# Gate/up in parts, two ff2 tiles after gru, and a split pointwise product in a one-core recurrent block

## The reference, cut to what matters

```
xn   = layernorm(x)
s    = recurrent(xn)      # conv + pointwise, minGRU, feed-forward, each with rmsnorm and residual
gate = fp4(xn) @ fp4(w_gate).T
up   = fp4(xn) @ fp4(w_up).T            # both 704 columns
h    = silu(gate) * up
g    = silu(fp4(h) @ fp4(w_down).T)
out  = x + s * g

def fp4(v):               # per block of 16 along the last dimension
    scale = max(max|v| / 6, 1e-12)
    return round_to_grid(v / scale, [0, .5, 1, 1.5, 2, 3, 4, 6]) * scale
```

## Time and profile before

| | us |
|---|---|
| median of 3 runs (lowest to highest) | 1191.91 (1191.78 to 1193.99) |
| the profiled execution | 1193.24 |
| its span, first to last instruction | 1191.2 |
| PE busy | 1102.8 (93%) |
| DVE busy | 865.2 (73%) |
| ACT busy | 549.9 (46%) |
| POOL busy | 143.1 (12%) |
| mean granted TensorE clock | 0.979 of full |

### The profile page before, as it was taken

How to read it: one execution, slowest core, us unless ns; L and a number is a source line. 1 busy time by engine, 2 the same in 40 slices (tenths; PEclk the granted TensorE clock), 3 DMA queues, 4 the chain that set the end, 5 groups by cost and what they waited for, 6 DMA issues and landing times.

```text
span 1191.2 us, 18158 instructions
## 1 busy us (share of the span) xinstructions
PE 1102.8 (93%) x6306; PEld 969.6 (81%) x6306; DVE 865.2 (73%) x1638; ACT 549.9 (46%) x887; POOL 143.1 (12%) x122
## 2 busy tenths in 40 slices
PE   3467999999999999999999999999999999999998
PEld 2355988879898888988888798987889888888987
DVE  5777686868868586885868678686777858777655
ACT  3235454454545455453545444454444434544441
POOL 3010020101102010110201011020201101020010
PEclk9587999999999999999999999999999999999999
DMA  6000000010101001010010101001010100100000
GB/s 225 1 0 18 19 27 28 1 55 1 36 18 34 22 1 53 1 36 20 1 53 1 54 1 36 19 1 55 1 36 17 36 19 1 53 1 18 18 19 18
DMA packets 29355, 31.46 MB, mean 26 GB/s; under 512 B 1120, under 2 KB 28512, under 8 KB 29280
## 3 DMA queue, kind: packets, MB, share of 16 engines
q1 hardware_dynamic: 20000, 21.04, 5.6%
q10 hardware_dynamic: 9280, 9.26, 2.4%
HBM read 21.90 MB, written 8.39 MB: 25 GB/s over the span
## 4 chain that ended last, share of the span: by engine, by line
PE 76%; DVE 15%; issue 4%; ACT 4%; DMA 0%; POOL 0%; DVEq 0%; ACTq 0%; POOLq 0%
PE gu_ps L855 39%; PE w_ps L855 26%; PE w_ps L918 3%; DVE hqt_lo L471 2%; DVE x L506 2%; DVE hq L393 2%; DVE q_amax L367 2%; PE gu_ps L901 1%; PE w_ps L862 1%; ACT hqt_hi L732 1%; PE w_ps L873 1%; PE gu_ps L862 1%; DVE q_y L379 1%; PE w_ps L901 1%; DVE cand L504 1%
## 5 line engine op out<-in xcount | busy, mean ns | idle before, releaser
L855 PE MATMUL w_ps<-w,act 128*128 128x256 f32 x960 | 217.1, 379 | 0.0
L455 DVE TENSOR_TENSOR hid<-sl,gu_ps 128x352 f32<-128x352 f32 x128 | 65.7, 514 | 189.2 <-ACT sl L721 189.1
L855 PEld LDWEIGHTS w_ps<-w,act 128*128 128x128 f32 x960 | 177.7, 190 | 21.7
L855 PE MATMUL gu_ps<-gu_hi,xq_hi 128*128 128x352 f32 x512 | 170.1, 332 | 10.5 <-issue 9.5
L855 PE MATMUL gu_ps<-gu_lo,xq_hi 128*128 128x352 f32 x512 | 166.7, 326 | 1.7 <-issue 1.6
L855 PE MATMUL gu_ps<-gu_hi,xq_lo 128*128 128x352 f32 x512 | 166.4, 325 | 0.0
L855 PE MATMUL w_ps<-dn_hi,hqt_hi 128*128 128x256 f32 x384 | 119.6, 312 | 8.6 <-DVE hqt_lo L471 8.6
L721 ACT ACTIVATE sl<-gu_ps 128x352 f32<-128x352 f32 x128 | 59.4, 464 | 133.9 <-PE gu_ps L855 133.5
L327 POOL TENSOR_TENSOR inv_rms<-ss_row,neg_half 128x4 f32<-128x4 f32 x32 | 40.6, 1270 | 596.3 <-DVE ss_row L481 596.3
L759 ACT ACTIVATE act<-gu_ps,cols 128x512 f32<-128x512 f32 x128 | 86.5, 688 | 54.7 <-PE gu_ps L855 54.6
L855 PE MATMUL gu_ps<-xs_hi,w_hi 128*128 128x512 f32 x256 | 106.2, 415 | 3.1 <-DVE xs_lo L495 3.1
(11 more groups left out here) (115 smaller groups left out, 2199.4 us busy)
## 6 DMA issues: line engine op xcount, KB each, us to landing
x_in<-x_dram SPq DMA_DIRECT2D x16, 512.0 KB, 4.5
x_res<-x_dram ACTq DMA_DIRECT2D x16, 512.0 KB, 3.5
out_dram<-o SPq DMA_DIRECT2D x15, 512.0 KB, 3.2
act<-w_t_dram SPq DMA_DIRECT2D x1, 1024.0 KB, 13.3
w<-w_t_dram SPq DMA_DIRECT2D x1, 1024.0 KB, 15.6
act<-w_down_dram SPq DMA_DIRECT2D x1, 704.0 KB, 10.3
hid<-w_gate_dram SPq DMA_DIRECT2D x1, 640.0 KB, 5.6
hid<-w_up_dram SPq DMA_DIRECT2D x1, 640.0 KB, 9.2
```

The lines of the kernel that those rows point to most:

```text
L455: V.tensor_tensor(hid[:, t, h * HALF:(h + 1) * HALF], sl[:, h, :], gu_ps[:, h, 1, 0:HALF], ALU.mult).then_inc(hid_ready, 1)
L855: done = M.matmul(psum, l, r, start=first and i == 0, stop=last and i == len(terms) - 1)
```

## The change

1. `gate_up(c, t, u)`: a call now does one part u (0 gate, 1 up) over all 704 columns, that is both halves, each half in a bank of its own. The bank indices are swapped to `gu_ps[:, u, h]`. The gate part waits for the silu of the tile before, the up part for its product. Silu and product are one instruction each for a tile, of 704 elements; the product waits for silu and for the up part. `silu_ready` and `hid_ready` count tiles and no longer halves.
2. `down(c-1, 2)` on PE goes behind both parts of gate/up of tile 3; on DVE `hidden_low(c-1, 2)` goes behind `hidden(c, 3)`, and the other steps of the section are reordered.
3. After `gru` come two tiles of ff2, then the sums of squares and `down(c-1, 3)`; ff2 of tile 3 then comes ahead of tile 2. On DVE both recurrences come ahead of `hidden_low(c-1, 3)`.
4. `pointwise(c+1)` is split: part 0, then `down(c, 0)`, then part 1.

```diff
@@ hidden, hidden_scales (DVE)
-            def hidden(c, t, h):
-                dve.wait_ge(silu_ready, 2 * T * c + 2 * t + h + 1)
-                V.tensor_tensor(hid[:, t, h * HALF:(h + 1) * HALF], sl[:, h, :],
-                                gu_ps[:, h, 1, 0:HALF], ALU.mult).then_inc(hid_ready, 1)
+            def hidden(c, t):
+                dve.wait_ge(silu_ready, T * c + t + 1)
+                dve.wait_ge(gu_done, 2 * (T * c + t) + 2)
+                V.tensor_tensor(hid[:, t, :].rearrange("p (h n) -> p h n", h=2), sl[:],
+                                gu_ps[:, 1, :, 0:HALF], ALU.mult).then_inc(hid_ready, 1)
@@ body (DVE)
-                hidden(c, 2, 0)
+                hidden(c, 2)
                 if tail:
                     hidden_values(c - 1, 2, rounded)
-                    scales = hidden_scales(c - 1, 3)
-                hidden(c, 2, 1)
-                if tail:
-                    ratios = fp4_ratios(hid[:, 3, :], NBI, scales)
-                    hidden_low(c - 1, 2)
                 else:
                     down_weight_low(0)
                     down_weight(1)
                 scaled(c * 2, x1, w_ps[:, 1, :], (x1_ready, KD * (c + 1)))
                 if tail:
+                    scales = hidden_scales(c - 1, 3)
+                scaled_low(c * 2)
+                if tail:
+                    ratios = fp4_ratios(hid[:, 3, :], NBI, scales)
                     dve.wait_ge(dve_step, ratios)
-                hidden(c, 3, 0)
-                scaled_low(c * 2)
-                if tail:
+                hidden(c, 3)
+                if tail:
+                    hidden_low(c - 1, 2)
                     rounded = fp4_round(NBI, ratios)
-                hidden(c, 3, 1)
-                if tail:
                     hidden_values(c - 1, 3, rounded)
...
                 recurrence(c, 0)
+                recurrence(c, 1)
                 if tail:
                     hidden_low(c - 1, 3)
-                recurrence(c, 1)
                 add_squares(c * 2 + 1)
@@ silu_gate (ACT)
-                for h in halves:
-                    n = 2 * T * c + 2 * t + h
-                    act.wait_ge(gu_done, n + 1)
-                    if not (isinstance(c, int) and n < 2):
-                        act.wait_ge(hid_ready, n - 1)
-                    A.activation(sl[:, h, :], gu_ps[:, h, 0, 0:HALF], ACT.Silu).then_inc(silu_ready, 1)
+                act.wait_ge(gu_done, 2 * (T * c + t) + 1)
+                act.wait_ge(hid_ready, T * c + t)
+                A.activation(sl[:], gu_ps[:, 0, :, 0:HALF], ACT.Silu).then_inc(silu_ready, 1)
@@ gate_up (PE)
+                elif u == 0:
+                    pe.wait_ge(silu_ready, T * c + t)
                 else:
-                    pe.wait_ge(hid_ready, n - 1)
+                    pe.wait_ge(hid_ready, T * c + t)
                 tok = slice(t * P, (t + 1) * P)
-                for u in range(2):
+                for h in range(2):
                     cut = slice(u * NI + h * HALF, u * NI + (h + 1) * HALF)
@@ body (PE)
                 gate_up(c, 3, 0)
+                gate_up(c, 3, 1)
                 if tail:
                     down(c - 1, 2)
-                gate_up(c, 3, 1)
-                if not tail:
+                else:
                     down_weight(1)
                 gru(c, 0)
                 gru(c, 1)
                 if tail:
                     hq_transposes(c - 1, 3, (g_ready, T * c - 1))
                     ff2(c - 1, 0, w_ps[:, 0, :], (ss_ready, 2 * c + 1))
+                    ff2(c - 1, 1, w_ps[:, 1, :], (xs_ready, KD * (2 * c + 1)))
+                sum_squares(c * 2 + 1, gu_ps[:, 0, 0, :], (coef_ready, KD * c + 1))
+                if tail:
                     down(c - 1, 3)
-                sum_squares(c * 2 + 1, gu_ps[:, 0, 0, :], (coef_ready, KD * c + 1))
-                if tail:
-                    ff2(c - 1, 1, w_ps[:, 1, :], (xs_ready, KD * (2 * c + 1)))
                 spread_scale(c * 2 + 1, gu_ps[:, 0, 1, :], (cand_ready, KD * c + 1))
                 if tail:
+                    ff2(c - 1, 3, w_ps[:, 3, :], (hqtlo_ready, T * c))
                     ff2(c - 1, 2, w_ps[:, 2, :], (g_ready, T * c))
-                    ff2(c - 1, 3, w_ps[:, 3, :], (hqtlo_ready, T * c))
...
                 if front:
-                    pointwise(c + 1)
+                    pointwise(c + 1, (0,))
                 down(c, 0, w_ps[:, 2 if front else 0, :])
+                if front:
+                    pointwise(c + 1, (1,))
```

More of the change, by code:

```diff
@@ L242, in mixed_recurrent_kernel, with ff2_place @@
                   .rearrange("p (k n) -> p k n", n=P))
+        def ff2_place(c, t):
+            return t + 1 if t < 2 or isinstance(c, int) and c == B - 1 else 6 - t
         def weight_places(p, dst):
@@ L573, in body @@
                     hidden_values(c - 1, 1, fp4_round(NBI, steps.base))
-                hidden(c, 0, 0)
-                hidden(c, 0, 1)
+                hidden(c, 0)
                 if tail:
                     scales = hidden_scales(c - 1, 2)
-                hidden(c, 1, 0)
                 add_squares(c * 2)
@@ L581, in body @@
                     hidden_low(c - 1, 1)
-                hidden(c, 1, 1)
+                hidden(c, 1)
                 if tail:
@@ L602, in body @@
                 if tail:
-                    dve.wait_ge(dve_step, ratios)
-                hidden(c, 3, 0)
+                    scales = hidden_scales(c - 1, 3)
                 scaled_low(c * 2)
                 if tail:
+                    ratios = fp4_ratios(hid[:, 3, :], NBI, scales)
+                    dve.wait_ge(dve_step, ratios)
+                hidden(c, 3)
+                if tail:
+                    hidden_low(c - 1, 2)
                     rounded = fp4_round(NBI, ratios)
-                hidden(c, 3, 1)
-                if tail:
                     hidden_values(c - 1, 3, rounded)
@@ L809, in body @@
                 high_part(c * 2, (ff1_done, KF * c))
-                silu_gate(c, 3, (0,))
+                silu_gate(c, 3)
                 if tail:
@@ L867, in front_xc, with pointwise @@
                     front_transposes(c, xc, xc_ready, k, w_ps[:, k, :], xct_done)
-            def pointwise(c):
-                for e in range(KD):
+            def pointwise(c, parts=range(KD)):
+                for e in parts:
                     pe.wait_ge(y_ready, KD * (c + 1))
@@ L885, in gate_up @@
                     pe.wait_ge(gelu_ready, KF * c)
+                elif u == 0:
+                    pe.wait_ge(silu_ready, T * c + t)
                 else:
-                    pe.wait_ge(hid_ready, n - 1)
+                    pe.wait_ge(hid_ready, T * c + t)
                 tok = slice(t * P, (t + 1) * P)
-                for u in range(2):
+                for h in range(2):
                     cut = slice(u * NI + h * HALF, u * NI + (h + 1) * HALF)
                     for k in range(KD):
-                        last = product(gu_ps[:, h, u, 0:HALF], (xq_hi[:, k, tok], xq_lo[:, k, tok]),
+                        last = product(gu_ps[:, u, h, 0:HALF], (xq_hi[:, k, tok], xq_lo[:, k, tok]),
                                        (gu_hi[:, k, cut], gu_lo[:, k, cut]), k == 0, k == KD - 1)
@@ L1031, in body @@
                     ff2(c - 1, 0, w_ps[:, 0, :], (ss_ready, 2 * c + 1))
-                    down(c - 1, 3)
+                    ff2(c - 1, 1, w_ps[:, 1, :], (xs_ready, KD * (2 * c + 1)))
                 sum_squares(c * 2 + 1, gu_ps[:, 0, 0, :], (coef_ready, KD * c + 1))
                 if tail:
-                    ff2(c - 1, 1, w_ps[:, 1, :], (xs_ready, KD * (2 * c + 1)))
+                    down(c - 1, 3)
                 spread_scale(c * 2 + 1, gu_ps[:, 0, 1, :], (cand_ready, KD * c + 1))
                 if tail:
+                    ff2(c - 1, 3, w_ps[:, 3, :], (hqtlo_ready, T * c))
                     ff2(c - 1, 2, w_ps[:, 2, :], (g_ready, T * c))
-                    ff2(c - 1, 3, w_ps[:, 3, :], (hqtlo_ready, T * c))
                 ff1(c, range(KF // 2))
```

18 lines of the change are left out of this document (8 added, 10 removed).

## The result

| | before | after |
|---|---|---|
| median of 4 runs each (us) | 1192.95 (1191.78 to 1194.89) | 1220.02 (1218.94 to 1221.21) |
| ratio, with 95% interval | | 1.0226 (1.0206 to 1.0245) |
| profiled execution (us) | 1193.24 | 1219.31 |
| its span (us) | 1191.2 | 1217.2 |
| mean granted TensorE clock | 0.979 | 0.973 |

What follows compares the result with a forecast made beforehand. PE's matmuls plus its waits were taken as the bound. Middle +30.5, loop end -7.0, chunk 0 -1.4, old fall -1.0 and clock +13.6 gave +34.7 on 1193.24, 1227.9; as median 1226.6 us, range 1207 to 1243.

Steps and rivals of the forecast that it cites:

- Place one: PE's transposes of hq of tile 2 wait for the whole tile's product on DVE; +1.61 us a chunk.
- Place two: PE's down of tile 2 waits for hqt_lo, now behind the product of tile 3; +2.11 us, old 0.73 goes.
- Sums: PE's wait for DVE before the sums of squares goes, a second ff2 tile covering it; -14.4 us.
- The spread: PE's step after the sums, now covered by down instead of ff2; stays in time with 0.4 us to spare.
- Loop end: At six jumps back, longer pointwise matmuls cover more of PE's branch; -1.17 us each, -7.0 in all.
- Chunk 0: Gru's wait for xs_lo in the first chunk ends earlier, as it no longer follows half a product; -1.4 us.
- The clock: New half-clock stretches after the idle before down of tile 2: eight at 1.7 us, +13.6 (0 to +26).
- the old fall: The one half-clock stretch behind a jump in the kernel before goes with the shorter idle; -1.0 us.
- DVE's 9 us less, worth 0: Merged instructions spare DVE 9 us, worth 0 because DVE is not the bound.
- Both waits, no falls: Rival: both new PE waits come but no new half-clock stretches; 1213.0 us, chance 0.17.
- One wait is hidden: Rival: hq of tile 2 is in time and costs nothing; 1188.8 us, chance 0.06 shared with grouping.
- Grouping wins: Rival: DVE is the bound, so merged instructions pay; some 1170 us, chance 0.06 shared with a hidden wait.

Runs made afterwards that it cites:

- a_lo: The changed kernel with hqt_lo of tile 2 moved on DVE ahead of the scales and the product of tile 3; 1179.51 us, 0.9880 of the kernel before.
- a_both: The changed kernel with both hq and hqt_lo of tile 2 moved on DVE ahead of the products they stood behind; 1154.62 us, 0.9673 of before.
- a_hq: The changed kernel with the values hq of tile 2 moved on DVE ahead of the product of tile 2; 1220.33 us, 1.0222 of before.
- a_half: The changed kernel with each tile's product as two instructions of 352, each started when its half of up is done; 1219.29 us, 1.0214 of before.
- b_ff2: The kernel before with only item 3 of the change, the new order behind gru; 1179.57 us, 0.9886 of before.
- b_pw: The kernel before with only the split pointwise product around down of tile 0; 1184.09 us, 0.9922 of before.
- both_half: a_both with each tile's product as two instructions of 352; 1155.31 us, 0.9677 of the kernel before.
- a_fill: The changed kernel with nine extra matmuls of 352 columns, result unread, ahead of down of tile 2; 1209.99 us, 1.0139 of before.
- lo_half: a_lo with each tile's product as two instructions of 352; 1172.22 us, 0.9824 of the kernel before.
- b_parts: The changed kernel with items 3 and 4 taken back, so items 1 and 2 alone; 1241.93 us, 1.0404 of the kernel before.
- both_jump: a_both with one k step of pointwise part 0 moved from ahead of down of tile 0 to behind it; 1153.02 us, 0.9664 of before.

## Why the prediction was right

The side, the mechanism and both new places came out as predicted. The time was 6.6 us high. The predicted change was 34.7 and the medians differ by 27.1, so the sum is 7.6 too large (1.0 of it does not show in the time, since the median of the kernel before was taken as 1191.91 and is 1192.95 in the result). Most of it is one term, the clock.

- **Place one**, +1.61 predicted: 1.59. The product of 704 elements, taken as 0.89 between 0.51 and 1.03, took 0.888. Shown causal by `a_lo` to `a_both`, -24.9 us.
- **Place two**, +2.11 predicted: 2.10. Shown by `after` to `a_lo`, -40.5 with its falls of the clock. The prediction's remark that DVE's steps between the places "just fit" was right by 0.28 us (the bracket at 643.32), and it mattered more than it said: in `a_hq` and `a_half` that slack was gone and the gain with it.
- **Sums**, -14.4: the wait is gone; `b_ff2` gives -14.3. The spread held with 665.57 - 665.07 - 0.15 = 0.35 to spare, for a predicted 0.4.
- **Loop end**, -1.17 a jump: -1.4, made of two things. At the jump itself the gain was about 0.9 (mean idle 1.58 before, 0.68 after), less than 1.17 because the branch grew, from 3.39 to 3.66 on the mean of the six; and the later issue wait of some 0.5, which the prediction never priced, also went. So the term came near by two errors that partly cancel. By the queue of 64 for PE that the Trainium skill states (TensorE: Matmul & The Clock Gate, Architectural detail, on engine queue depths), an estimate of 32 pairs of weight load and matmul, there would have been nothing to gain there. The traces do not agree: sixteen matmuls were left at each of the jumps, and `b_pw` is 9.8 us faster.
- **Chunk 0**, -1.4: shown. Gru starts 2.63 behind the start of the six transposes ahead of it, where it was 4.02. The next chunk starts 2.0 earlier, but the other 0.6 is not the change's: with the same chunk 0 it starts at 120.5 in `a_both` and 122.5 in `a_lo`, and the mean granted clock from 25 to 115 us is 0.75 in the one and 0.73 in the other (0.75 after, 0.73 before).
- **The clock**, +13.6 from eight falls at 1.7: this is the mis-sized term. It was six falls, and each cost some 1.5, not 1.7: 9.0, or 4.6 less. Both were estimates, the price from half of the stretch, the number a guess between 0 and 15 for which no row had a reason: that the time came this near is luck in this term. With the other differences (0.5 less for the two places, 1.4 more for the jumps, 0.6 for the start, 0.1 for the old fall) 34.7 becomes the 27.5 of the tally.
- **DVE's 9 us less, worth 0**: DVE has 9.3 less, and `both_half` shows that it is worth nothing measurable.
- **The rivals.** "Both waits, no falls" (1213) is what `a_fill` shows from the other side: without falls 1210. "One wait is hidden" asked for `hq` in time, and `a_hq` shows that even then there is no gain, since place two grows; its 1188.8 had held place two at 2.11 and left the coupling out. "Grouping wins": the Trainium skill (Perfetto Trace Analysis, Optimizing Scalar/DVE Operations) says that where ScalarE or VectorE is not saturated but causes bubbles on other engines, breaking up its instructions may get work done sooner; `lo_half` agrees, with 5.5 us less of waits from splitting the product that PE waits for, and `both_half`, +0.7 and unresolved, fits too, since there is no bubble there.

## What to carry to other kernels

When two instructions are merged or reordered on a helper engine, what counts is what now stands behind the merged one and who waits for it: the same change gave +27 us with two DVE steps behind the product and -39 us with them ahead. Before taking a wait away, look at the slack of the same engine at the next place; fifteen waits of 1.6 us were removed here for nothing. A change with a bad total can hold good parts, so time each part alone: two of three were worth 24 us.

## What the runs showed of the hardware

- **Idle time and the clock.** Idle as drawn ahead of `down(2)`, and falls of the granted clock to 0.52 behind it in the 15 chunks: 2.7 us, 15 falls (`a_hq`); 1.94 us, 6 (after) and 3 (`b_parts`); 1.95 us, 10 (`a_half`); 0.5 to 0.6 us, none (`a_fill`, before). At place one 1.42 brought none in any kernel. `b_parts` had two more falls, behind jumps with 1.94 and 2.16 of idle. But length alone does not decide: the same 1.94 brought a fall in some chunks and none in others, 1.77 at a jump was followed by a fall once in the kernel before, and `b_ff2` had 1.96 (2.0 in this view) at a jump with none:

```profile
PE gu_ps L859 <- issue: 11.3, 9, 2.0
```

What else plays in was not tested. The counts are those of one traced execution each; the granted clock of the others is near it in most kernels (0.972 to 0.973 after, 0.980 to 0.982 `a_fill`), but runs from 0.975 to 0.980 in `b_ff2`. Work whose result nobody reads can be worth its while there (`a_fill`, -10.0 us).

- **The loop's branch on PE** took 3.3 to 3.9 us at the median: 3.34 before and `a_fill`, 3.52 `b_pw`, 3.55 `a_both`, 3.69 after, 3.86 `both_jump`. Why it differs is open. Sixteen matmuls were left to start when it began, at every jump of every kernel. What can be had is cover: the longer the matmuls that stand last in the turn, the less of it shows.
